# Whole-row accumulating scatters, ordered by expert, in a routed feed-forward stage

## The reference

```python
scores = softmax(einsum('bsh,he->bse', layernorm(x), G))      # 8 experts
value, indices = top_k(scores, 2)                             # each row goes to 2 of them
w = einsum('bsk,bske->bse', value, one_hot(indices, 8))
gated = silu(x @ gate_w[e]) * (x @ up_w[e])                    # 128 wide, plus a rank-16 branch
out = sum over e of w[e] * (gated @ down_w[e] + lora[e])
x = x + tanh(g_ffn) * out
```

## Time and profile before

| of the profiled execution | |
|---|---|
| time of that run, its span | 1570.3 us, 1568.5 us |
| median of three other runs | 1568.64 us |
| PE, DVE, ACT, POOL busy over the span | 1426.0, 1148.1, 774.6, 1177.9 us |
| share of the chain that ended last: DMA out<-made,dest | 15% |
| DMA, mean over the span | 201 GB/s |
| slot stage: first and last HT transposes on PE | 1081.9 and 1543.5 us |

### The profile page before, as it was taken

The page is one execution under the profiler, slowest core; times in us unless marked ns, Lnnn a source line. Parts: engine busy times, 40 slices in busy tenths (PEclk is TensorE's granted clock), DMA queues, the critical chain, the costliest instruction groups (busy, mean ns, idle before and its releaser), DMA issues. The chain is left out here.

```text
span 1568.5 us, 33155 instructions
## 1 busy us (share of the span) xinstructions
PE 1426.0 (91%) x10482; PEld 1380.1 (88%) x10483; DVE 1148.1 (73%) x1913; ACT 774.6 (49%) x1359; POOL 1177.9 (75%) x765
## 2 busy tenths in 40 slices
PE   4999999999999999999999999545998988989994
PEld 4999999999999999999999999445988877888883
DVE  3999999999999999999999999582444444444442
ACT  5665656656665565566657565102333333333331
POOL 6989888898988989889898887043656566565664
PEclk9999999999999999999999999657999999999997
DMA  5766667676676766767666675164999999999996
GB/s 193 229 201 226 203 216 223 208 231 201 215 225 207 227 200 223 217 207 229 207 221 211 209 227 187 53 196 109 174 224 222 199 214 229 196 215 230 170 171 88
DMA packets 124431, 314.97 MB, mean 201 GB/s; under 512 B 26160, under 2 KB 26672, under 8 KB 124400
## 3 DMA queue, kind: packets, MB, share of 16 engines
q1 hardware_dynamic: 93728, 239.83, 49.6%
q0 software_dynamic: 30672, 74.75, 24.4%
HBM read 215.37 MB, written 100.73 MB: 202 GB/s over the span
## 5 line engine op out<-in xcount | busy, mean ns | idle before, releaser
L532 DVE TENSOR_REDUCE oT<-z 128x128 f32<-128x1280 f32 x256 | 380.6, 1487 | 7.8
L633 PE MATMUL Y<-kvhi,t_hi 128*128 128x288 f32 x1280 | 382.6, 299 | 0.0
L634 PE MATMUL Y<-kvlo,t_hi 128*128 128x288 f32 x1280 | 377.8, 295 | 0.0
L635 PE MATMUL Y<-kvhi,t_lo 128*128 128x288 f32 x1280 | 377.1, 295 | 0.0
L1081 POOL DMA_INDIRECT out<-made,dest x142 | 222.3, 1566 | 164.6 <-DMA out<-made,dest 115.4
L307 POOL TENSOR_TENSOR kvlo<-kv,kvhi 128x1152 fp32r<-128x1152 f32 x128 | 340.7, 2683 | 0.0
L290 POOL TENSOR_TENSOR kv<-cT 128x768 f32<-128x768 f32 x128 | 236.5, 1847 | 8.4 <-DMA cT<-in_c 8.4
L634 PEld LDWEIGHTS Y<-kvlo,t_hi 128*128 128x128 f32 x1280 | 241.0, 188 | 0.0
L635 PEld LDWEIGHTS Y<-kvhi,t_lo 128*128 128x128 f32 x1280 | 241.0, 188 | 0.0
L633 PEld LDWEIGHTS Y<-kvhi,t_hi 128*128 128x128 f32 x1280 | 240.7, 188 | 0.0
L515 DVE TENSOR_TENSOR z<-Y,qT 128x512 f32<-128x512 f32 x256 | 176.9, 691 | 50.6 <-PE Y L635 41.8
(11 more groups left out here) (162 smaller groups left out, 3337.9 us busy)
## 6 DMA issues: line engine op xcount, KB each, us to landing
cT<-in_c SPq DMA_DIRECT2D x32, 768.0 KB, 8.1
t_hi<-khi SPq DMA_DIRECT2D x64, 384.0 KB, 3.8
t_lo<-klo SPq DMA_DIRECT2D x64, 384.0 KB, 5.0
u_hi<-kshi SPq DMA_DIRECT2D x64, 320.0 KB, 5.9
u_lo<-kslo SPq DMA_DIRECT2D x64, 320.0 KB, 6.9
x_nat<-in_x SPq DMA_DIRECT2D x32, 512.0 KB, 4.2
out<-x_new SPq DMA_DIRECT2D x32, 512.0 KB, 4.9
normed<-n SPq DMA_DIRECT2D x32, 512.0 KB, 7.6
```

The lines of the kernel that those rows point to most:

```text
L532: nc.vector.tensor_reduce(oT[p][:, 2 * r:2 * r + 2, h * IB:(h + 1) * IB], view(z[s][:], [[ZC, 2], [2, IB], [2 * IB, ZS], [1, 2]]), AX.XY, ...
L633: nc.tensor.matmul(out, w_hi[:, w], m_hi[:, c, :], start=start, stop=False)
L634: nc.tensor.matmul(out, w_hi[:, w], m_lo[:, c, :], start=False, stop=False)
L635: return nc.tensor.matmul(out, w_lo[:, w], m_hi[:, c, :], start=False, stop=stop)
```

## The change

Four things are changed. A scatter moves whole rows of 1024 columns, so there is one of them in a slot and not two. It no longer waits for the scatter of the slot before it; a table `need`, made by DVE, says for each slot and each of four semaphores (`scattered[b]`, slot k counting on number k mod 4) how far it must have counted for all slots of preceding experts to have landed. Within an expert that number is reached before the second slot comes, so its scatters may overlap, up to the four buffers; an empty slot waits for all slots before it. To keep the awaited numbers above zero, four small DMAs at the start of `route_tokens` bring each semaphore to 16. And a row of `normed` is 1040 numbers long where it was 1032 (the 8 weights behind the row have 8 zeros beside them).

```diff
-RW = L + E
+RW = L + 2 * E
@@ route_tokens, DVE
                 V.memset(weights.lb[:].bitcast(F32), 0.0).then_inc(weights.lb_zero, 1)
+                link(V.memset(wt[:], 0.0))
+                for b in range(NB):
+                    link(V.memset(shift[:, b, :], float(NB - 1 - b)))
...
                 V.tensor_tensor(keep.own[:], expert[:].rearrange("p (s o) -> p s o", o=1).to_broadcast([P, SG, E]),
                                 iota[:, 0:E].rearrange("p (o e) -> p o e", o=1).to_broadcast([P, SG, E]), ALU.is_equal)
+                link(V.tensor_tensor(last[:], ended[:, :, E - 1:E].rearrange("p s o -> p (s o)"), grid[:], ALU.mult))
+                link(V.tensor_tensor(ended[:], ended[:], end.rearrange("p (o e) -> p o e", o=1).to_broadcast([P, SG, E]), ALU.mult))
+                link(V.tensor_reduce(began[:], ended[:], AX.X, ALU.max))
+                link(V.tensor_tensor(began[:], began[:], last[:], ALU.max))
+                link(V.tensor_tensor(need_i[:], shift[:], began[:].rearrange("p (o s) -> p o s", o=1).to_broadcast([P, NB, SG]),
+                                     ALU.add))
+                link(V.tensor_scalar(need_i[:], need_i[:], NB.bit_length() - 1, None, ALU.logical_shift_right))
+                V.tensor_scalar(keep.need[:], need_i[:], 16.0, 16.0, ALU.mult, ALU.add)
                 eng.wait_ge(idx_done, 1)
                 V.tensor_scalar(keep.token[:], IDX[:, 0:SG], -1.0, 0.0, ALU.add, ALU.max).then_inc(token_done, 1)
@@ route_tokens, POOL
+                for b in range(NB):
+                    eng.dma_start(keep.opened[0:1, b, :], normed_d[0:1, 0:E]).then_inc(keep.scattered[b], 16)
@@ experts_on_slots, POOL
                 def scatter(k):
-                    for c in range(2):
-                        eng.wait_ge(d_out[c], k + 1)
-                        if k:
-                            eng.wait_ge(scattered[c], 16 * k)
-                        eng.indirect_dma_start(out=rows_d,
-                                               out_offset=bass.IndirectOffsetOnAxis(ap=keep.dest[c][:, k:k + 1], axis=0),
-                                               in_=made[k % NB][:, c * HALF:(c + 1) * HALF], in_offset=None,
-                                               compute_op=ALU.add).then_inc(scattered[c], 16)
+                    need = [eng.value_load(keep.need[0:1, b, k:k + 1], min_val=1, max_val=16 * (BACK + 2)) for b in range(NB)]
+                    for b in range(NB):
+                        eng.wait_ge(scattered[b], need[b])
+                        nc.gpsimd.tensor_tensor(clear[:, NB * k + b:NB * k + b + 1], keep.own[0:1, k, 0:1], keep.own[0:1, k, 0:1], ALU.mult)
+                    eng.wait_ge(d_out[0], k + 1)
+                    eng.wait_ge(d_out[1], k + 1)
+                    eng.indirect_dma_start(out=rows_d,
+                                           out_offset=bass.IndirectOffsetOnAxis(ap=keep.dest[:, k:k + 1], axis=0),
+                                           in_=made[k % NB][:], in_offset=None, compute_op=ALU.add).then_inc(scattered[k % NB], 16)
...
@@ ACT and DVE, before they write made[q]
-                        eng.wait_ge(scattered[0], 16 * (k - NB + 1))
+                        eng.wait_ge(scattered[q], 4 * (k - q) + 16)
```

More of the change, by code:

```diff
@@ L756, in __init__ @@
         U32 = mybir.dt.uint32
-        self.token = sb("token", [P, SG], U32)
-        self.dest = [sb(f"dest{c}", [P, SG], U32) for c in range(2)]
+        self.token, self.dest = sb("token", [P, SG], U32), sb("dest", [P, SG], U32)
+        self.need = sb("need", [P, NB, SG], mybir.dt.int32)
+        self.opened = sb("opened", [1, NB, E])
+        self.scattered = [ctx.enter_context(nc.semaphore(f"scattered{b}")) for b in range(NB)]
         self.own = sb("own", [P, SG, E])
@@ L825, in route_tokens @@
         sc, ta, tb = sb("sc", [P, NT, E]), sb("ta", [P, NT, E]), sb("tb", [P, NT, E])
-        wt = sb("wt", [P, NT, E])
+        wt = sb("wt", [P, NT, 2 * E])
         oh = [sb(f"oh{c}", [P, NT, E]) for c in range(2)]
@@ L840, in route_tokens @@
         expert, spare = sb("expert", [P, SG]), sb("spare", [P, SG])
-        row_at = sb("row_at", [P, SG])
+        began, last, shift = sb("began", [P, SG]), sb("last", [P, SG]), sb("shift", [P, NB, SG])
+        need_i = sb("need_i", [P, NB, SG], I32)
         CNT, IDX = ps("CNT", [P, HALF]), ps("IDX", [P, HALF])
@@ L904, in _ @@
                 eng.wait_ge(misc, 3)
-                link(V.scalar_tensor_tensor(out=wt[:], in0=chosen[:].bitcast(F32), scalar=gt[:, 0:1], in1=sc[:],
+                link(V.scalar_tensor_tensor(out=wt[:, :, 0:E], in0=chosen[:].bitcast(F32), scalar=gt[:, 0:1], in1=sc[:],
                                             op0=ALU.mult, op1=ALU.mult), "weights")
@@ L947, in _ @@
                 link(V.tensor_scalar(spare[:], IDX[:, 0:SG], 0.0, number[:, NT:NT + 1], ALU.is_equal, ALU.mult))
-                link(V.scalar_tensor_tensor(out=row_at[:], in0=IDX[:, 0:SG], scalar=-1.0, in1=spare[:], op0=ALU.add, op1=ALU.add))
-                for c in range(2):
-                    V.tensor_scalar(keep.dest[c][:], row_at[:], 2.0, float(c), ALU.mult, ALU.add)
+                V.scalar_tensor_tensor(out=keep.dest[:], in0=IDX[:, 0:SG], scalar=-1.0, in1=spare[:], op0=ALU.add, op1=ALU.add)
             @block.sync
@@ L993, in _ @@
                 eng.wait_ge(weight_out, 16)
+                for b in range(NB):
+                    eng.wait_ge(keep.scattered[b], 16)
                 eng.wait_ge(token_done, 1)
@@ L1056, in experts_on_slots @@
         wrow_done = sem("wrow_done")
-        scattered = [sem(f"scattered{c}") for c in range(2)]
+        scattered = keep.scattered
+        clear = sb("clear", [1, SLOTS * NB])
         def table(kind, k):
@@ L1093, in _ @@
                 scatter(SLOTS - 1)
-                for c in range(2):
-                    eng.wait_ge(scattered[c], 16 * SLOTS)
+                for b in range(NB):
+                    eng.wait_ge(scattered[b], 16 * ((SLOTS - 1 - b) // NB + 2))
             @block.scalar
@@ L1147, in row_weight @@
                     at = slice(k, k + 1) if isinstance(k, int) else bass.ds(k, 1)
-                    nc.vector.scalar_tensor_tensor(out=own_weight[q][:], in0=xr[q][:, L:RW], scalar=1.0,
+                    nc.vector.scalar_tensor_tensor(out=own_weight[q][:], in0=xr[q][:, L:L + E], scalar=1.0,
                                                    in1=keep.own[:, at, :].rearrange("p o e -> p (o e)"), op0=ALU.mult,
@@ L1160, in copy_out @@
                     if not (isinstance(k, int) and k < NB):
-                        eng.wait_ge(scattered[1], 16 * (k - NB + 1))
+                        eng.wait_ge(scattered[q], 4 * (k - q) + 16)
                     nc.vector.tensor_scalar(made[q][:, HALF:L], D[1][:], wrow[q][:, 0:1], None, ALU.mult).then_inc(d_out[1], 1)
@@ L1297, in build @@
         experts_on_slots(nc, keep, constants, weights, rows, whi, wlo, bhi, blo, normed,
-                         out.rearrange("t p l -> (t p) l").rearrange("r (c l) -> (r c) l", c=2))
+                         out.rearrange("t p l -> (t p) l"))
 def kernel(**inputs):
```

## The result

The changed kernel takes 1528.58 us (median of 4 runs, 1527.41 to 1529.94), the kernel before beside it 1570.14 us (4 runs): ratio 0.9738 (95%: 0.9713 to 0.9762). The profiled execution has a span of 1527.8 us, 40.7 less than before.

A forecast was written before the change was run, and what follows sets the result against it. PE was taken to bound the slot stage, stalling 44.6 us on gathers held behind chained scatters on POOL. From a span of 1568.5 us, -34.6 (stall), -1.8 (tail) and +3.7 (routing) gave 1536 us, range 1518 to 1570.

The forecast's parts named there:

- Part 1, the stall: Slot stage: without the scatter chain within an expert, PE loses most of its 44.6 us of stall; -34.6 us.
- The 10 us that I left for DMA-bound stretches: Slot stage: stall expected to stay of the 44.6 us, a quarter; bounds 0, and 30 if a row costs 0.47.
- The loads counted hidden: Slot stage, POOL's sequencer: four register loads, 1.8 us a slot, cost nothing because the sequencer runs ahead of the engine.
- a sign of being wrong: TENSOR_LOADs on POOL's sequencer with POOL idle behind them in every slot would show loads in series.
- the 3.9 of my sum: POOL's work a slot: 3.2 us for gather, scatter and gaps plus 0.75 for four small operations, 2 us under PE.
- Part 2, the wait between experts: Each expert's first scatter, seven times: POOL comes 1 us late and wins it back, costing PE nothing; 7 us without cover.
- Part 3, the tail: Kernel's end: empty slots 68 to 70 stay a chain of 7.0 us links, 23.2 us for 25.0; -1.8 us.
- Part 4, routing: End of the routing stage: memsets 1.0 us and seven operations before `token` 2.7 us delay the first gathers; +3.7 us.
- DMA becomes the limit: Rival, slot stage: whole rows cost 0.47 us, overlapping scatters only queue, 30 us of stall stay; 1556 us, chance 0.13.
- POOL in series: Rivals, slot stage: register loads add to POOL's slot time; 1549 us if cheap (0.07), 1591 or 1633 if dear (0.10).
- still one by one: Rival, slot stage: scatters still land one by one, 7.0 us a slot, 490 for 461.6; 1599 us, chance 0.02.
- nothing gained: Rival, slot stage: gathers wait in the same DMA rings behind whole-row scatters, stalls stay; 1568 to 1572 us, chance 0.06.

The follow-up runs named there:

- serial_whole: The changed kernel, but each whole-row scatter waits for the scatter of the slot before it: 1582.91 us, 1.0110 of the kernel before.
- half_overlap: The changed kernel, but each scatter is two halves of 512 columns again, both under the table of counts: 1537.21 us, 0.9825 of the kernel before.
- two_in_flight: The changed kernel, but a scatter also waits for the one two slots before: 1528.65 us, 0.9767 of the kernel before.
- route_hidden: The changed kernel with the table's seven operations put behind `token` and `dest`, and the memsets (`wt`'s cut to its zeros) in waits of DVE: 1524.60 us, 0.9727.
- narrow_rows: The changed kernel with rows of `normed` of 1032 numbers again and without the memset of the 8 zeros: 1529.43 us, 0.9762 of the kernel before.
- best_late: The changed kernel with `route_hidden`, four spare output tiles for empty places, three register loads a slot, and first four gathers behind the stage barrier: 1512.91 us, 0.9654.
- best_last: `best_late` with the operations that make the table of counts also moved behind the barrier between the two stages: 1511.76 us, 0.9657 of the kernel before.

## Why the prediction was right, and which terms were off

Forecast 1536 us, range 1518 to 1570, faster 0.82; measured 1528.58. The mechanism was the one forecast: PE stalled on gathers that stood behind a chain of scatters, and without the chain PE runs at its own pace. `serial_whole` puts the chain back and the stall with it. The total is 7.4 us under the forecast, since a term of the stall that was too careful outweighs one of the routing that was too small.

- *Part 1, the stall: -34.6 forecast, -45.0 measured.* The 10 us that I left for DMA-bound stretches are the mis-sized term; nothing stayed. The whole-row scatter costs 0.43 us a packet (52.8% of 27 us for 2.18 MB, queue q0 in 1493:1520), for my 0.40, and the DMA work is 0.90 x 423 = 381 us for my 390. That the two agree is in part luck. With 0.43 my own sum gives 430 - 71 x (16 x 0.235 - 8 x 0.43) = 407 us, and `half_overlap`, which moves the half rows of before, has 0.95 x 418 = 397 us of work for 430. A packet thus has no fixed price here, and what sets it stays open. What the work costs PE was sized wrong: even at a share of 1.01 PE lost nothing in a weight load. Half rows under the same table, with a share of 0.95, put HT 1.6 us further apart than whole rows, in their fastest run.
- *The loads counted hidden: right, though not as I had it.* The trace shows four loads in up to 3.4 us of sequencer time beside the gather's descriptors, not 1.8, and POOL idle behind them in 61 slots. I had named that idle time as a sign of being wrong, and it came. It costs nothing: where POOL is late its loads start early, take 1.9 us, and a slot takes 3.7 to 4.2 us, for the 3.9 of my sum. What I didn't see is how little more would break it: with two more loads a slot of POOL's takes 5.81 us, and PE begins to stall.
- The Trainium skill's floor of about 600 ns for a register load ("DMA: Bandwidth & Descriptors", "Latency and other measured facts") is not what one instruction shows here (0.296 us median), but four of them with their register operations took 3.4 us beside a gather, more than its 2.4.
- *Part 2, the wait between experts: nothing, as forecast*; 11 waits of 25.8 us with those of the empty slots, and level again after one slot of 3.8 us (forecast 3.9).
- *Part 3, the tail: -1.8 forecast, -3.4 measured.* The four scatters start at -9.3, -2.2, 4.7 and 11.2 us from the last HT, forecast -9.5, -2.5, 4.5 and 11.5. The rest is what follows the last one's start: 10.4 us, for my 5.8 to the landing and 5.9 behind it. That sum took the DRAIN of 5.44 us as fixed; it took 4.07. In all 13 kernels POOL's last DRAIN ends 8.5 to 9.0 us behind the end of the last scatter's descriptors, whenever it starts, so a scatter that lands later (whole rows) makes it shorter and the end no later.
- *Part 4, routing: +3.7 forecast, +7.7 measured.* The routing itself came out: the memsets took 1.5 us for 1.0 (the four of `shift` 0.18 each) and the seven operations 2.4 for 2.7, so that `token` starts 966.7 us behind the first block's first product to L711, for 962.9 before: +3.8. Another 1.8 us were there before that: this product starts at 96.5 and not 94.7. It belongs to this execution and not to the change, since in the 11 other changed kernels it starts at 94.7 to 96.2. The last 2.1 us came behind `token`: the drain ended 6.4 us later than before, and slot 0's HT a further 1.3. The prediction put nothing there; `two_in_flight`, whose routing is the same, shows 1.2 of them. `route_hidden` brought `token` to 962.7 us behind the first product, and its median is 4.0 us lower than the changed kernel's, 4.8 lower than that of `narrow_rows` in its own group.
- *Rivals.* "DMA becomes the limit" falls with the weight-load row, where PE is busy throughout at a share of 1.01; "POOL in series" with `half_overlap`, where the engine does 1.9 us more a slot and HT stands 418.2 us apart; "still one by one" is what `serial_whole` is, at 6.70 us a link and not 7.0; "nothing gained" falls with the wait for `slot_rows`, which is gone.

## What to carry to other kernels

Where DMAs are ordered only because some of them might touch the same place, order the groups that might and let the rest overlap: here two in flight were enough, and without the overlap the larger transfer lost. Register loads on POOL cost nothing here while they fitted in front of the next gather, and 0.5 to 1.0 us of its pace each beyond that; try the addition doubled, and by half, to see how much room is left. Read an engine's own pace where nothing holds it up, behind a wait, and not in a slot where it follows another engine. What builds the table of an ordering belongs behind the value that the next stage waits for, and what a drain would wait for belongs behind the barrier.

## What the runs showed of the hardware

A DMA share of 1.01 did not mean lost time: with more in flight the same engines moved 270 GB/s for 256 in a weight load, and PE never waited. And a TENSOR_LOAD on POOL took 0.28 us at the least and up to 1.53 us; in the slots looked at, the long ones lie beside the gather's descriptors or right behind them. POOL's DRAIN took 8.3 to 9.8 us at the routing stage's end in all 13 kernels, and 4.1 to 5.5 us at the program's end. Its end follows the engine's last instruction, not its own start: 0.4 us behind a tensor operation (`best_late`, `best_last`), 4.9 to 5.9 us behind the last of four gathers, 8.5 to 9.0 us behind the last scatter. What it waits for behind the DMAs was not tried.
